# Attention heads on one core: P-tiles of rows 8 to 15 transposed as 32x32 blocks and moved by DMAs, with a head's last weighted sums in the next head

## The reference

```python
xn = _layernorm(x, axis=-1)
# attention, 16 heads of size 128
k = einsum('ihd,bpd->biph', W_K, xn); q, v alike
scores = einsum('biph,biqh->biqp', k, q)        # causal mask, then / sqrt(128)
attn = softmax(masked, axis=-1)
z = einsum('biqp,biph->biqh', attn, v)
out_a = einsum('df,bqf->bqd', W_O, z_flat)
# feed-forward, hidden 1024
hidden = fwht(silu(xn @ W1.T) * (xn @ W3.T));  out_f = hidden @ W2.T
return x + out_a + out_f
```

## Time and profile before

| | us |
|---|---|
| median of 3 runs | 1655.33 (1654.64 to 1655.88) |
| profiled execution, span | 1653.5 |
| TensorE busy in it | 1590.5 (96%) |
| VectorE busy | 1088.2 (66%) |
| ScalarE busy | 958.8 (58%) |
| GpSimd busy | 261.4 (16%) |

### The profile page before, as it was taken

How to read it: one execution, slowest core, us unless ns; L and a number is a source line. 1 busy time by engine, 2 the same in 40 slices (tenths; PEclk the granted TensorE clock), 3 DMA queues, 4 the chain that set the end, 5 groups by cost and what they waited for, 6 DMA issues and landing times.

```text
span 1653.5 us, 31426 instructions
## 1 busy us (share of the span) xinstructions
PE 1590.5 (96%) x10536; PEld 1428.3 (86%) x10536; DVE 1088.2 (66%) x2776; ACT 958.8 (58%) x2071; POOL 261.4 (16%) x209
## 2 busy tenths in 40 slices
PE   4999999999999999999999999999999999999998
PEld 3888898998989898988989898989989898989987
DVE  6433675858667675858677675758576676758585
ACT  3322474756657574746567474747566574747565
POOL 4200111212121211112021202112021212112111
PEclk7999999999999999999999999999999999999999
DMA  3000000000000000000000000000000000000000
GB/s 129 26 1 0 1 1 14 0 0 13 0 13 0 13 0 13 0 1 13 0 13 0 13 0 13 0 13 0 0 13 0 13 0 13 0 13 0 0 20 33
DMA packets 7259, 16.65 MB, mean 10 GB/s; under 512 B 512, under 2 KB 4736, under 8 KB 6784
## 3 DMA queue, kind: packets, MB, share of 16 engines
q1 hardware_dynamic: 7168, 15.80, 2.9%
HBM read 13.70 MB, written 2.10 MB: 10 GB/s over the span
## 4 chain that ended last, share of the span: by engine, by line
PE 91%; issue 4%; DVE 2%; ACT 2%; DMA 1%; DVEq 0%; SPq 0%; POOL 0%; POOLq 0%
PE ps L738 25%; PE ps L740 25%; PE ps L739 25%; PE ps L864 14%; PE ps L879 2%; DMA probs<-w1t 1%; ACT q_hi L421 1%; DVE z_lo L673 0%; DVE w_raw L520 0%; DVE ps L637 0%; ACT probs L446 0%; DVE pt_lo L555 0%; DVE neg_max L648 0%; DVE stats L534 0%; ACT pt_hi L381 0%
## 5 line engine op out<-in xcount | busy, mean ns | idle before, releaser
L428 ACT CAST pt_hi<-ps 128x512 fp32r<-128x512 f32 (+3 forms) x640 | 320.5, 525 | 237.0 <-PE ps L864 230.5
L655 DVE TENSOR_TENSOR pt_lo<-ps,pt_hi 128x512 fp32r<-128x512 f32 (+3 forms) x640 | 369.4, 606 | 41.5 <-ACT pt_hi L428 34.2
L446 ACT ACTIVATE probs<-ps,neg_max 128x1024 f32<-128x1024 f32 (+9 forms) x384 | 332.8, 871 | 89.2 <-DVE neg_max L648 84.8
L642 DVE TENSOR_REDUCE bank_max<-ps 128x1 f32<-128x512 f32 x384 | 264.7, 689 | 139.0 <-PE ps L740 137.0
L864 PE MATMUL ps<-ident,probs 128*128 128x128 f32 x2176 | 321.9, 274 | 30.3 <-ACT probs L446 30.2
L738 PE MATMUL ps<-pt_hi,v_hi 128*128 128x256 f32 (+1 forms) x1152 | 339.2, 294 | 2.6 <-DVE z_lo L673 2.6
L331 POOL TENSOR_TENSOR acc<-w_a,acc 128x512 f32<-128x512 f32 x128 | 164.3, 1284 | 1106.3 <-ACT w_a L462 1106.3
L740 PE MATMUL ps<-pt_hi,v_lo 128*128 128x256 f32 (+1 forms) x1152 | 324.5, 282 | 0.0
L739 PE MATMUL ps<-pt_lo,v_hi 128*128 128x256 f32 (+1 forms) x1152 | 324.5, 282 | 0.0
L864 PEld LDWEIGHTS ps<-ident,probs 128*128 128x128 f32 x2176 | 256.5, 140 | 71.0 <-issue 33.5
L738 PE MATMUL ps<-k_hi,q_hi 128*128 128x512 f32 (+3 forms) x640 | 251.5, 393 | 0.0
(11 more groups left out here) (95 smaller groups left out, 2215.8 us busy)
## 6 DMA issues: line engine op xcount, KB each, us to landing
w_raw<-w_heads SPq DMA_DIRECT2D x16, 512.0 KB, 3.3
acc<-x SPq DMA_DIRECT2D x4, 512.0 KB, 11.4
out<-acc SPq DMA_DIRECT2D x8, 256.0 KB, 2.1
w_a<-w2t SPq DMA_DIRECT2D x1, 1024.0 KB, 8.2
probs<-w1t SPq DMA_DIRECT2D x1, 1024.0 KB, 11.2
probs<-w3t SPq DMA_DIRECT2D x1, 1024.0 KB, 13.2
w_b<-hadamard SPq DMA_DIRECT2D x1, 64.0 KB, 3.2
```

Source lines behind the costliest of these rows:

```text
L428: act.copy(pt_hi4[:, (j // 2) % 2, 4 * g:4 * g + n, (j % 2) * P:(j % 2 + 1) * P], bank(ring_bank((j, g)), 0, n * P).rearrange("p (t q) -> ...
L446: act.activation(probs[:, j % 2, b * BANK:b * BANK + n], ps[:, at:at + n], ACT.Exp, bias=neg_max[:, j:j + 1], accum_out=row_part[:, j, e:e ...
L642: dve.tensor_reduce(bank_max[:, j, b:b + 1], ps[:, at:at + n], AX_X, ALU.max).then_inc(maxed, 1)
L655: dve.tensor_tensor(pt_lo4[where], bank(ring_bank((j, g)), 0, n * P).rearrange("p (t q) -> p t q", q=P), pt_hi4[where].bitcast(F32), ALU.s ...
```

## The change

Chunks 4 to 7 (rows 8 to 15) no longer go through TensorE and PSUM for their transposes. Chunks 0 to 3 do as before.

- ScalarE writes the exponentials of a moved row in blocks of 32 keys, the two rows of a chunk interleaved, so that 64 neighbouring numbers hold one block of both.
- VectorE transposes all 32x32 blocks of a row in place, one instruction per row (`transpose_blocks`), after all exponentials of that row. It stands behind the first bank maximum of the next row.
- SP moves a chunk from `probs` to `pt_lo` in 16 DMAs (`move`), one for each pair of 32-partition groups, in pieces of 64 numbers (256 bytes). It waits for the blocks and for the weighted sum of chunk c - 2, whose place in `pt_lo` it takes.
- ScalarE copies `pt_lo` to `pt_hi` in pieces of four key tiles, 128x1024 (`moved_to_hi`), 14 pieces per head; GpSimd subtracts in place (`moved_to_lo`), also 14.
- The sums of chunks 6 and 7, and the outputs of chunks 5 to 7, run in the next pass of the head loop. A last, 17th pass holds only those of head 15.
- Q is projected slice by slice into the ring and kept for two slices; only one buffer `v_raw` is left. K is projected at the start of a pass, no longer at the end of the one before.

```diff
+            def move(h, c):                                      # SP
+                sp.wait_ge(blocked, place_free(h, c))
+                sp.wait_ge(z_product, place_free(h, c))
...
+                src = probs[:, at:at + n * CHUNK_Q].rearrange("p (i b x) -> p i b x", b=4, x=2 * BLK)
+                dst = pt_of(pt_lo, c).rearrange("p i (a x) -> p i a x", a=4)
+                for b in range(4):
+                    for a in range(4):
+                        sp.dma_start(dst[b * BLK:(b + 1) * BLK, :, a, :].bitcast(F32),
+                                     src[a * BLK:(a + 1) * BLK, :, b, :]).then_inc(moved[c % 2], 16)
...
+            def moved_to_lo(h, c, g):                            # GpSimd
+                pool.wait_ge(new_hi, piece_count(h, c, g))
+                pool.tensor_tensor(lo, lo.bitcast(F32), hi.bitcast(F32), ALU.subtract).then_inc(new_lo, 1)
...
+                if j == 14 and e == 1:                           # ScalarE, exponential
+                    act.wait_ge(moved[1], moved_count(h, 5))
...
+            def moved_to_hi(h, c, g):
+                if g == 0:
+                    act.wait_ge(moved[c % 2], moved_count(h, c))
+                act.copy(pt_of(pt_hi, c)[:, a:b, :], pt_of(pt_lo, c)[:, a:b, :].bitcast(F32)).then_inc(new_hi, 1)
...
+            def transpose_blocks(h, j):                          # VectorE
+                dve.wait_ge(exped, EX[TILES] * h + EX[j + 1])
+                v = moved_probs(j // 2)[:, 0:4 * (j + 1), j % 2, :]
+                ins = dve.transpose(v, v)
...
+            def period(h, first, last):                          # TensorE; first and last leave parts out
+                project_k(h, 0); project_q(h, 0); project_k(h, 1); project_k(h, 2); project_k(h, 3)
+                scores(h, 0); scores(h, 1); output(h - 1, 5); weighted_sum(h - 1, 6, 0, 8)
+                scores(h, 2); scores(h, 3); weighted_sum(h - 1, 6, 8, 14)
+                transposes(h, 0); transposes(h, 1); project_q(h, 1); scores(h, 4)
+                output(h - 1, 6); weighted_sum(h - 1, 7, 0, 8); scores(h, 5); weighted_sum(h - 1, 7, 8, 16)
+                project_v(h, 0); transposes(h, 2); transposes(h, 3); transpose_v(h, 0); project_v(h, 1)
+                output(h - 1, 7); transpose_v(h, 1); project_v(h, 2); scores(h, 6); transpose_v(h, 2)
+                project_v(h, 3); weighted_sum(h, 0, 0, 2); transposes(h, 4); transposes(h, 5)
+                transpose_v(h, 3); output(h, 0); weighted_sum(h, 1, 0, 4); project_q(h, 2)
+                scores(h, 7); transposes(h, 6); transposes(h, 7); scores(h, 8)
+                output(h, 1); weighted_sum(h, 2, 0, 6); scores(h, 9); weighted_sum(h, 3, 0, 4)
+                scores(h, 10); output(h, 2); weighted_sum(h, 3, 4, 8); scores(h, 11); project_q(h, 3)
+                scores(h, 12); output(h, 3); scores(h, 13); weighted_sum(h, 4, 0, 6)
+                scores(h, 14); weighted_sum(h, 4, 6, 10); scores(h, 15); output(h, 4)
+                weighted_sum(h, 5, 0, 12)
```

More of the change, by code:

```diff
@@ L38 @@
 CHUNK_Q = 256
+BLK = 32
 EPS = 1e-5
@@ new lines, in period @@
+                if not last:
+                    exps(h, 5)
+                if not first:
+                    moved_to_hi(h - 1, 7, 3)
+                    z_to_hi(h - 1, 7)
+                if not last:
+                    p_to_hi(h, 2)
+                    p_to_hi(h, 3)
+                    v_to_hi(h, 0)
+                if not first:
+                    output(h - 1, 7)
+                if last:
+                    return
+                v_to_hi(h, 1)
+                exps(h, 6)
+                v_to_hi(h, 2)
@@ L507, in _ @@
[L507 to L509 removed]
+            period(0, True, False)
+            with act.Fori(1, HEADS) as h:
+                period(h, False, False)
+            period(HEADS, False, True)
         @block.vector
@@ new lines, in negated_maximum, with row @@
+            def negated_maximum(h, j):
+                dve.wait_ge(maxed, HEAD_BANKS * h + TB[j + 1])
+                dve.tensor_reduce(neg_max[:, j:j + 1], bank_max[:, j, 0:banks_of(j)], AX_X, ALU.max,
+                                  negate=True).then_inc(negmaxed, 1)
+            def row(h, j, first=0, last=None):
+                for b in range(first, banks_of(j) if last is None else last):
+                    maximum(h, j, b)
+                if last is None:
+                    negated_maximum(h, j)
@@ new lines, in output @@
+            def output(h, c):
+                pe.wait_ge(z_lo_done, chunk_count(h, c))
+                ring_wait(h if c < PREV_O else h + 1, ("O", c))
+                if c == 0:
+                    pe.wait_ge(wo_split, h + 1)
+                for t in range(2):
+                    qs = slice(t * P, (t + 1) * P)
+                    ins = mm3(bank(ring_bank(("O", c)), t * D, (t + 1) * D), (z_hi[:, qs], z_lo[:, qs]),
+                              (wo_hi[:, :], wo_lo[:, :]), True, True)
+                ins.then_inc(wo_product, 1)
@@ L958, in head @@
[L958 to L968 removed]
+                    transposes(h, 0)
+                    transposes(h, 1)
+                    project_q(h, 1)
+                    scores(h, 4)
@@ new lines, in period @@
+                if not first:
+                    output(h - 1, 6)
+                    weighted_sum(h - 1, 7, 0, 8)
+                if not last:
+                    scores(h, 5)
+                if not first:
+                    weighted_sum(h - 1, 7, 8, 16)
+                if last:
+                    output(h - 1, 7)
+                    return
+                project_v(h, 0)
+                transposes(h, 2)
+                transposes(h, 3)
+                transpose_v(h, 0)
+                project_v(h, 1)
@@ new lines, in period @@
+                if not first:
+                    output(h - 1, 7)
+                transpose_v(h, 1)
+                project_v(h, 2)
+                scores(h, 6)
+                transpose_v(h, 2)
+                project_v(h, 3)
+                weighted_sum(h, 0, 0, 2)
+                transposes(h, 4)
+                transposes(h, 5)
+                transpose_v(h, 3)
+                output(h, 0)
+                weighted_sum(h, 1, 0, 4)
+                project_q(h, 2)
+                scores(h, 7)
```

868 lines of the change are left out of this document (499 added, 369 removed), and 3 rows, old and new, of the table ITEMS.

## The result

The changed kernel takes **2128.9 us** (median of 4 runs, 2128.3 to 2129.6) against 1655.3 before: ratio 1.286, 95% interval 1.284 to 1.288. Forecast was 2080, range 1940 to 2280. Slower, as said, by 29% where 26% was forecast; the time also lies in the prediction's own narrower range, 1990 to 2170.

What follows compares the result with a forecast made beforehand. TensorE's in-order work bounded the old kernel; waits make the changed head 118.2 us. 175.5 before head 0, 96.7 for head 0, 1773 for heads 1 to 15 and 34 for the last pass, plus 1.8, give 2080 us; range 1940 to 2280.

Steps and rivals of the forecast that it cites:

- What goes: In rows 8 to 15, 100 TensorE transposes per head, 11.0 us; 78.1 us of its work stays.
- the first rival: "TensorE stays the bound": over the whole head, waits add up to less than 14 us; 1480 us, chance 0.07.
- TensorE busy below 75%: Sign listed for the forecast being right, beside a head period near 118 us.
- the check of the walk: Over one head, TensorE's work of 78.1 us plus its waits gives 116.1, beside the chain's 116.3.
- Block transposes: VectorE's in-place transpose of row j: 1.35 us (row 8) to 2.28 (row 15), 14.5 per head.
- the second rival: Block transposes at half the assumed rate, in rows 8 to 14: + 11.2 us a head, 2260 us, chance 0.13.
- Chain (d): Rows 9 to 15: maximum, exponentials, block transpose, next row's other banks run in sequence; 46.3 us to the next K.
- (a): Head's start, 0 to 19.9 us: scores 4 wait 1.6 us for the low part of Q slice 1.
- (b): Weighted sum 7: first piece waits 4.8 us, later ones 1.0, 1.2 and 2.8; ends at 36.5 us.
- Scores 12: Step from row 11 to 12: Q slice 3 is copied and subtracted first, so TensorE waits 6.4 us.
- the third rival: DMAs outrun their cover, from about 16 us per chunk on; put at 2400 us, chance 0.09.
- The clock: TensorE at 1.2 GHz after long waits costs only where TensorE is awaited: +1.9 us a head, ends 0 and +9.

Runs made afterwards that it cites:

- e2: Changed kernel with each block transpose of rows 8 to 14 moved behind the whole maximum of the next row; 2030.0 us.
- e3: Changed kernel with block transposes of only 128 numbers per row, the rest left out, waits kept; 2018.0 us.
- e6: Changed kernel with unread filler matmuls added in TensorE's waits before weighted sum 7, before its last four tiles and before scores 12; 2079.8 us.
- e4: Changed kernel with ScalarE's four copies of chunk 7 put ahead of the exponentials of rows 4 and 5 (two each); 2004.7 us.
- e5: Changed kernel with Q slice 3 projected behind scores 7 instead of before scores 12, its copy and subtraction earlier too; 2076.7 us.
- e7: Changed kernel with half of the moved blocks left out, 8 DMAs a chunk instead of 16; 2123.3 us.
- e8: Changed kernel with the edits of e1, e2, e4 and e5 together; 1872.3 us.
- e9: e8 with scores 14 put ahead of weighted sum 4; 1864.8 us.
- e11: e9 with half of the moved blocks left out, 8 DMAs a chunk instead of 16; 1778.6 us.
- e1: Changed kernel with VectorE's sum of two partial row sums written as a one-operand reduction; 2109.6 us.
- e12: e9 with GpSimd's subtraction over half of the columns of every moved piece; 1791.5 us.

## Why the prediction was right, and where it was off

- **What goes** was right in kind: TensorE has less work, and it is worth nothing, since the waits of a head are far above the 14 us that the first rival needed. "TensorE stays the bound" fell with the waits. The sign named for it, TensorE busy below 75%, was missed by two points.
- **Work and waits of TensorE**: the check of the walk, 78.1 us of work and 38.0 of waits a head, came near the 116.3 of the chain by luck. Measured are 92.7 us busy and 28.1 idle (120.80 - 92.74). The three windows at half clock hold 14.7 us of busy time, of which about half, 7 us by estimate, would go at full clock; what makes the rest was not told apart.
- **Block transposes**: 1.37 to 2.31 us, the taken value; the second rival (half rate) fell.
- **Chain (d)**, the core of the argument: 46.3 forecast, 46.4 measured from row 9 to K, each step within 0.8. e2 and e3 show that the transposes' length stands in it. It was right because nearly every term was a row of before and every queue was followed in order. The closeness is in part luck: e6 takes 0.6 us out of these steps, so 46.4 holds some of the clock, which the walk adds apart.
- **(a) and (b)**: waits of 1.42 and 4.48 for 1.6 and 4.8. e4 shows the cause of the 4.48 to be ScalarE's order: 8.5 us a head.
- **Scores 12** (6.4 forecast, 5.7 came): e5.
- **DMAs**: the step that was wrong and did no harm. 10 us a chunk were taken; chunk 7's packets alone take 13.1, and 14.4 pass from the first issue to the last packet. Issues are slower than 0.50 (0.67 to 0.71), and a 256 B packet takes 26 ns of an engine in chunks 4 to 6 and 31 in chunk 7: 9.8 GB/s (256 B by 26 ns) where 2.2 KB at 0.107 us make 20.6. The Trainium skill ("DMA: Bandwidth & Descriptors", Specifications) says that below 512 B a DMA engine reads, modifies and writes, which the prediction took as making 6.4 us into 13; the measured 13.1 agrees in size, but a fixed price per packet would fit as well, and no run tells the two apart. In chunks 4 to 6 it is the issues that set the length: chunk 4 has 320 packets an engine, 8.3 us at 26 ns, and took 10.7, as 16 issues 0.67 apart do. Cover of 18 us (1001.9 to 1020.2) kept it hidden (e7), as the third rival's point of 16 would have it. Once e8 had shortened the head, the DMAs did outrun their cover (e8, e9 and e11).
- **The clock** is the term that was mis-sized: 1.9 us a head forecast, at least 3.4 by e6. I counted half rate "only where TensorE is awaited" and overlooked that the stretch behind (b) covers the V slices, where TensorE is the bound, and that the eight tiles before scores 5 delay the last copy of chunk 7.
- **The row sum** was missing: 1.7 us a head (e1). VectorE was counted as free of GpSimd.
- **The sum.** K of head 0 at 174.5 (forecast 175.5), head 0 97.2 (96.7), fifteen heads of 121.2 (118.2), the last pass 38.4 (34): -1.0 + 0.5 + 44.4 + 4.4 = 48 us, which is 2127.5 less 2079. Without its clock term the walk has 116.3; clock 3.4 and row sum 1.7 make it 121.4, where 121.2 came. The two were measured apart and may overlap, so the 121.4 is no proof that nothing else is in it.

## What to carry to other kernels

Work moved off the busiest engine pays only where its new path fits beside the old one: walk every in-order queue that it joins, and add the waits of a head before crediting the work saved. Where a wait goes, ask at once which buffer or transfer is next; here half of the DMAs were worth 5.6 us in one order and 86 in a better one. Before naming what a wait comes from, take out the suspect and see in which step the time is gained: e12 gained, but not where it was looked for. And a wait on TensorE costs more than its length when the work behind it runs at 1.2 GHz.

## What the runs showed of the hardware

- A VectorE instruction with two operands in SBUF is held until GpSimd's running `pt_lo` subtraction, itself one with two operands there, ends: 0.15 us became up to 2.35, and 0.15 again with one operand (e1). The Trainium skill ("SBUF — State Buffer", "SBUF: two separate sides") has this as an exclusive lock held for the whole instruction; the trace agrees. Block transposes, which read one operand, kept their length beside GpSimd (1.90 us at 1095.80 while GpSimd ran from 1096.36; all 16 of a length agree within 0.01 us).
- 256 B pieces from SBUF to SBUF moved at 9.8 GB/s for each of 16 DMA engines, half the 20.6 GB/s of the packets of the kernel before (2.2 KB on average), and at 26 to 27 ns a packet whether 8 or 16 DMAs a chunk were issued (chunk 7 with 16: 31).
- TensorE fell to 1.2 GHz four times in every head from the second on: near the start of weighted sum 7, before its last tiles, before scores 12, and a fourth time that alternates from head to head between scores 8, about 65 us into the head, and scores 15, at 111. Each time it was in a wait or within 1 us behind one, for 3.4 or 6.8 us.
